# Second layer of an AdaLN and mixture-of-experts kernel: products of the dense expert cut in quarters, all gathers ahead of the scatters, two experts spread by matmuls

## What is computed

```python
def _L1_ffn_ref(x, Wg, W1, b1, W2, b2):        # x: 4 x 256 x 128, 8 experts, FF = 512
    n = b * l                                   # 1024 tokens
    k = min(max(int(n * C / e), 1), n)          # 256 tokens for each expert
    S = jax.nn.sigmoid(xt @ Wg).T
    G, I = jax.lax.top_k(S, k)                  # each expert takes its best 256 tokens
    ex = xt[I]
    hid = jax.nn.gelu(jnp.einsum('ekh,ehf->ekf', ex, W1) + b1[:, None, :], approximate=False)
    out = (jnp.einsum('ekf,efh->ekh', hid, W2) + b2[:, None, :]) * G[..., None]
    new_x = jnp.zeros_like(xt).at[I.reshape(-1)].add(out.reshape(-1, h))
    return new_x.reshape(b, l, h)
```

## Time and profile before

| what | value |
|---|---|
| median of 3 runs | 166.43 us (164.91 to 167.19) |
| the profiled execution | 165.73 us |
| its span, first to last instruction | 163.8 us |
| around the span | 1.93 us |
| PE busy in the span | 139.5 us (85%) |
| DVE, ACT, POOL busy | 90.4, 82.0, 61.8 us |
| mean granted clock of PE | 0.968 |

### The profile page before, as it was taken

The page is one execution under the profiler, slowest core; times in us unless marked ns, Lnnn a source line. Parts: engine busy times, 40 slices in busy tenths (PEclk is TensorE's granted clock), DMA queues, the critical chain, the costliest instruction groups (busy, mean ns, idle before and its releaser), DMA issues.

```text
span 163.8 us, 3459 instructions
## 1 busy us (share of the span) xinstructions
PE 139.5 (85%) x1050; PEld 120.0 (73%) x1050; DVE 90.4 (55%) x304; ACT 82.0 (50%) x246; POOL 61.8 (38%) x65
## 2 busy tenths in 40 slices
PE   7999839999998999997899787799889988699500
PEld 3848339999997999853889666689879868599500
DVE  0279564566543555333698877674414954357732
ACT  1677516667775666500586789631254553560000
POOL 0000376555375455444000000014775877764000
PEclk9999986999999999999999999999999999999965
DMA  5993315999997871117109904000212064366434
GB/s 163 375 401 116 81 50 164 411 388 386 392 384 222 245 281 33 36 48 216 42 0 363 397 14 136 0 6 17 51 51 55 32 180 109 117 179 171 130 117 128
DMA packets 20531, 27.38 MB, mean 167 GB/s; under 512 B 2050, under 2 KB 14722, under 8 KB 20130
## 3 DMA queue, kind: packets, MB, share of 16 engines
q1 hardware_dynamic: 17570, 22.78, 41.1%
q0 software_dynamic: 1856, 3.86, 7.6%
q10 hardware_dynamic: 1088, 0.52, 1.1%
HBM read 20.57 MB, written 6.59 MB: 166 GB/s over the span
## 4 chain that ended last, share of the span: by engine, by line
PE 50%; DMA 18%; DVE 10%; POOL 8%; issue 6%; ACT 5%; DVEq 1%; ACTq 0%; POOLq 0%
PE bank L561 12%; PE bank L571 10%; PE bank L723 6%; PE bank L705 5%; DMA xs<-rows,gidx 5%; POOL plane L450 4%; DMA plane<-x_sb,idx 3%; PE bank L473 3%; DMA w_sb<-plane 2%; DMA got<-picked 2%; DMA xg<-rows,idx 2%; PE bank L605 2%; POOL xg L443 2%; PE bank L681 2%; DMA rows<-c_tok 2%
## 5 line engine op out<-in xcount | busy, mean ns | idle before, releaser
L829 ACT ACTIVATE hT<-bank,w_now 128x128 f32<-128x128 f32 x92 | 26.2, 367 | 14.1 <-PE bank L561 14.1
L561 PE MATMUL bank<-xg,w_now 128*128 (+1 forms) x184 | 26.2, 289 | 0.0
L417 POOL DMA_INDIRECT xs<-rows,gidx x16 | 15.9, 991 | 27.3 <-DMA rows<-c_tok 18.3
L906 ACT ACTIVATE h1T<-bank,c_sb 128x256 f32<-128x256 f32 x44 | 18.3, 470 | 13.4 <-PE bank L705 13.4
L571 PE MATMUL bank<-w_sb,hT 128*128 (+1 forms) x184 | 24.5, 276 | 0.3 <-ACT hT L829 0.3
L561 PEld LDWEIGHTS bank<-xg,w_now 128*128 128x128 f32 x184 | 23.9, 203 | 0.4 <-issue 0.2
L723 PE MATMUL bank<-v_sb,h1T 128*128 128x128 f32 x176 | 22.7, 280 | 1.0 <-ACT h1T L906 1.0
L571 PEld LDWEIGHTS bank<-w_sb,hT 128*128 128x128 f32 x184 | 22.5, 192 | 0.5 <-ACT hT L829 0.5
L723 PEld LDWEIGHTS bank<-v_sb,h1T 128*128 128x128 f32 x176 | 21.2, 192 | 2.0 <-ACT h1T L906 1.7
L422 POOL DMA_INDIRECT picked<-y,sidx x16 | 15.3, 959 | 13.2 <-DVE y L1076 12.0
L450 POOL DMA_INDIRECT plane<-x_sb,idx x12 | 14.1, 1175 | 6.5 <-DVE x_sb L1235 4.1
(11 more groups left out here) (195 smaller groups left out, 216.1 us busy)
## 6 DMA issues: line engine op xcount, KB each, us to landing
v_sb<-in_v SPq DMA_DIRECT2D x16, 256.0 KB
cw_sb<-in_cond_w SPq DMA_DIRECT2D x8, 386.5 KB
plane<-y SPq DMA_DIRECT2D x6, 512.0 KB, 5.5
w_sb<-plane SPq DMA_DIRECT2D x6, 512.0 KB, 4.2
w_sb<-in_w SPq DMA_DIRECT2D x2, 1024.0 KB, 9.5
w_sb<-in_w SPq DMA_DIRECT2D x1, 1290.0 KB, 7.4
w_sb<-in_w SPq DMA_DIRECT2D x1, 774.0 KB, 4.3
rows<-row SPq DMA_DIRECT2D x1, 544.0 KB, 3.4
```

What stands on the lines that cost most here:

```text
L417: pool.indirect_dma_start(out=xs[:, b % RING], out_offset=None, in_=rows0, in_offset=rows_at(gidx, b)).then_inc(gathered[b % RING], 16)
L561: mm = pe.matmul(bank[2 + j % 2][:, P * f:P * f + P], w1_now[:, j % WB_RING, P * f:P * f + P], xsT[:, bass.ds((j - e) * P, P)], start=True ...
L829: ins = act.activation(hT[:, j % 2, P * f:P * f + P], bank[2 + j % 2][:, P * f:P * f + P], ACT.Relu, bias=w1_now[:, j % WB_RING, F + f:F + ...
L906: act.activation(h1T[:, n % 2, fc], bank[UP_BANKS[(2 * n + h) % 4]][:, CAP * f:CAP * f + CAP], ACT.Gelu, bias=c1_sb[:, e * NF + fc:e * NF ...
```

## The change

1. **Quarters.** `up1` can do one of its two matmuls alone. The two of `up1(0, 0)` go into the last two turns of the gated MLP's loop (b = 9 and 10). `up1(2, 0)`, `up1(2, 1)` and `up1(3, 0)` are halved, and the halves stand on the two sides of a `count_experts` or of `spread_tau`. The wait for the weights (`in_v`) moves ahead of the loop. The units' PSUM banks and those of `turn_scores` change with it.
2. **Order of the dense stage.** `up1(1, 1)`, `up1(2, 1)`, `down_e(0, 1)` stand earlier; `down_e(1, 0)` moves from ahead of `count_ahead` to behind it; `turn_xg(0)` moves ahead of `down_e(3, 1)` and `find_slots(4)`. On ACT `gelu(0, 0)` moves ahead of the 1024-wide pass (L921), `take_scores(1)` moves behind the fourth sign count, and ACT makes the first half of `hlfv`, which DVE made (L1203).
3. **Gathers.** All 14 gathers stand ahead of the first scatter.
4. **Experts 5 and 6 spread.** 5 planes in place of 6, 10 scatters in place of 12, 4 one-hot matrices and 4 x 8 matmuls of `spread_out` in place of 2 and 2 x 8. The planes are taken at `{4: 0, 5: 1, 6: 2}`.

The core of the diff:

```diff
-PLANES = 6
+SPREADS = 4
+PLANES = 5
@@
-        GATHERS_AHEAD = 5
+        GATHERS_AHEAD = SPARSE
+        SCATTERS = NH * SPARSE - SPREADS
+        SUM_BANKS = (5, 3)
@@
-        TAKEN_AT = {3: 0, 4: 1, 6: 2}
-        UP_BANKS = (4, 5, 2, 3)
+        TAKEN_AT = {4: 0, 5: 1, 6: 2}
+        UP_BANKS = (2, 4, 5, 3)
+        SCORE_BANKS = (0, 7)
@@ POOL, add(e)
-                for h in range(NH):
+                for h in range(min(NH, SCATTERS - NH * e)):
@@ PE
+            def up1(n, h, parts=(0, 1)):
...
+                for f in parts:
...
+            pe.wait_ge(in_v, 16 * 2 * E)
             for b in range(NC + 3):
...
+                if b > NC:
+                    up1(0, 0, (b - NC - 1,))
                 if 0 <= b - 3 < NC:
                     turn_d(b - 3)
@@ PE, spread_out
+                for n in range(SPREADS):
+                    e, h = (SCATTERS + n) // NH, (SCATTERS + n) % NH
+                    pe.wait_ge(spread_ready, n + 1)
                     pe.wait_ge(y1_kept, NH * e + h + 1)
@@ PE
-            up1(1, 0)
+            up1(1, 1)
+            up1(2, 0, (0,))
             count_experts(2)
+            up1(2, 0, (1,))
             down_e(0, 0)
             count_experts(3)
-            up1(1, 1)
+            down_e(0, 1)
+            up1(2, 1, (0,))
             count_experts(4)
-            down_e(0, 1)
+            up1(2, 1, (1,))
+            up1(3, 0, (0,))
             count_experts(5)
-            up1(2, 0)
             spread_tau()
+            up1(3, 0, (1,))
+            count_ahead()
             down_e(1, 0)
-            count_ahead()
...
@@ ACT
             take_scores(0)
+            gelu(0, 0)
             act.wait_ge(first_tau, 1)
             act.activation(rest, scT, ACT.Identity, bias=tau[:], scale=-1.0).then_inc(rest_ready, 1)
-            gelu(0, 0)
-            take_scores(1)
...
+            act.wait_ge(hlf1h_ready, 1)
+            act.activation(hlfv[:, :, :, 0].rearrange("p c e h -> p (c e) h"), hlf1h[:], ACT.Identity,
+                           scale=const("pcol")).then_inc(hlfv_ready[0], 1)
@@ DVE
-            v.wait_ge(hlf1h_ready, 1)
-            v.tensor_scalar(hlfv[:, :, :, 0].rearrange("p c e h -> p (c e) h"), hlf1h[:], const("pcol"), None,
-                            ALU.mult).then_inc(hlfv_ready[0], 1)
```

More of the change, by code:

```diff
@@ L394, in _ @@
             for e in range(PLANES):
-                sp.wait_ge(added[e], 16 * NH)
+                sp.wait_ge(added[e], 16 * min(NH, SCATTERS - NH * e))
                 load(part[e].rearrange("p (c d) -> p c d", d=C), plane[e].rearrange("(c p) d -> p c d", p=P), part_in[e])
@@ L626, in turn_d @@
                 pe.transpose(bank[6][:, 0:P], dT[:, P * b:P * b + P], ident).then_inc(d_turned, 1)
+            def up1(n, h, parts=(0, 1)):
+                dense, e, q = unit[n]
+                rows_in = dT[:, CAP * q:CAP * q + CAP] if dense else xgT[:, e % 2]
+                if not dense:
+                    pe.wait_ge(xgT_ready, e + 1)
+                u = 2 * n + h
+                if u >= 4:
+                    pe.wait_ge(h1T_ready, 2 * (u - 4) + 2)
+                for f in parts:
+                    fc = 2 * h + f
+                    mm = pe.matmul(bank[UP_BANKS[u % 4]][:, CAP * f:CAP * f + CAP], v1_sb[:, e, P * fc:P * fc + P],
+                                   rows_in, start=True, stop=True)
+                    if f == 1:
+                        mm.then_inc(h1_ready, 1)
             pe.wait_ge(in_gw, 32)
+            pe.wait_ge(in_v, 16 * 2 * E)
             for b in range(NC + 3):
@@ L644, in turn_scores @@
                     pe.wait_ge(scT_ready, c + 1)
-                    mm = pe.transpose(bank[2 + g][:, P * (c % 4):P * (c % 4) + P], scT[:, P * c:P * c + P], ident)
+                    mm = pe.transpose(bank[SCORE_BANKS[g]][:, P * (c % 4):P * (c % 4) + P], scT[:, P * c:P * c + P], ident)
                 mm.then_inc(s_turned, 1)
@@ L691, in turn_xg @@
                 mm.then_inc(xg_turned, 1)
[L693 to L707, removed]
             def down_e(n, h):
@@ L761, in _ @@
             find_slots(1)
-            up1(3, 1)
+            down_e(2, 1)
             find_slots(2)
-            down_e(2, 1)
+            down_e(3, 0)
             find_slots(3)
-            down_e(3, 0)
+            turn_xg(0)
+            down_e(3, 1)
             find_slots(4)
-            down_e(3, 1)
-            turn_xg(0)
             up1(HEAD, 0)
@@ L888, in take_scores @@
                 act.wait_ge(s_turned, g + 1)
[L889 removed]
+                first_of_each = bank[SCORE_BANKS[g]][:].rearrange("p (c e j) -> p c e j", c=4, j=NJ)[:, :, :, 0]
                 act.activation(sc[:, 4 * g:4 * g + 4], first_of_each, ACT.Copy)
@@ L929, in _ @@
             count_signs(4)
+            take_scores(1)
             count_signs(5)
@@ L1219, in spread_rows @@
                 v.wait_ge(iota_ready, 1)
-                link(v.tensor_copy(idx1f[:], idx1[:, PLANES * NH:SPARSE * NH]))
-                for h in range(NH):
-                    v.tensor_scalar(spread1h[h], iota_t, idx1f[:, h:h + 1], None, ALU.is_equal).then_inc(spread_ready, 1)
+                link(v.tensor_copy(idx1f[:], idx1[:, SCATTERS:NH * SPARSE]))
+                for n in range(SPREADS):
+                    v.tensor_scalar(spread1h[n], iota_t, idx1f[:, n:n + 1], None, ALU.is_equal).then_inc(spread_ready, 1)
             def with_bias(n, h):
@@ L1275, in _ @@
                 v.wait_ge(summed, g + 1)
-                v.tensor_tensor(acc[:, 512 * g:512 * g + 512], acc[:, 512 * g:512 * g + 512], bank[2 + g][:],
+                v.tensor_tensor(acc[:, 512 * g:512 * g + 512], acc[:, 512 * g:512 * g + 512], bank[SUM_BANKS[g]][:],
                                 ALU.add).then_inc(out_ready, 1)
```

32 lines of the change are left out of this document (15 added, 17 removed).

## The result

The changed kernel took 158.01 us in the median of 4 runs (157.73 to 158.72), the kernel before 165.94 us on the same chip (4 runs, 164.91 to 167.19). The ratio is 0.9526 with a 95% interval of 0.9446 to 0.9605. The profiled execution took 158.72 us with a span of 156.9. Forecast were 159.9 us for the median, with a range of 158.0 to 163.0, and 157.3 for the span.

The account below looks back on a forecast made before the run. PE's products and POOL's indirect DMAs bounded the kernel, POOL's last scatter setting the end. PE's end, 153.93 - 4.15 + 3.72 = 153.5, put the last addition 6.5 us earlier: span 157.3, execution 159.2, median 159.9 us, range 158.0 to 163.0.

Parts of the forecast that it names:

- signs that were named: Expected in the trace: no PE row waits from expert 3, first slots near 109.7, DVE's last addition released by PE.
- 157.9 us: Whole kernel: the low case, if the scatters are quick and the quarters give their full 0.95 us.
- Dense stage: After the last count: tau's turn, count_ahead and hlfv come earlier; first slots at 109.7, not 110.51, 0.8 us gained.
- rival C: Dense stage gives nothing, as a count or threshold is delayed; everything starts 0.8 us later, 160.7 us; chance 0.09.
- Gathers ahead: PE's expert turns: expert 2's 1.6 us earlier, expert 6's at 136.7 in place of 140.86, 4.15 us gained.
- More spreading: PE's tail: two more blocks of 16 records add 3.72 us, so PE ends at 153.5.
- Fewer scatters: POOL's tail: at 1.175 us each, the tenth scatter starts at 142.6 and its plane is added at 152.2.
- The rule weighed: GpSimd contends with DVE for SBUF, so two more wide one-hots beside scatters speak against the change; sum left unchanged.
- A: Tail: the scatters' route ends last, at 1.8 us from scatter to scatter; about 162.1 us as a median; chance 0.22.
- B: Gathers land after 4.0 us in place of 2.6, so all of PE comes 1.4 later; 161.3 us; chance 0.07.
- D: PE's clock falls at the wait ahead of expert 2's turn and stays down; at worst 192.7 us; chance 0.02.
- E: Tail: DVE's sum or the output's transfer doesn't move up although PE and POOL do; about 165 us; chance 0.05.

Follow-up runs that it names:

- e3: The kernel before with all gathers ahead and experts 5 and 6 spread, but the old dense stage: 159.64 us, ratio 0.9714.
- r0: The changed kernel run again, unedited, on a chip where the kernel before took 181.17 us: 170.46 us, ratio 0.95.
- e1: The changed kernel with the gathers of experts 5 and 6 behind scatters again and planes taken as before: 159.85 us, ratio 0.9707.
- e5: The kernel before with all gathers ahead of the scatters and planes taken as in the change, nothing else: 175.87 us, ratio 0.9752 (slower chip).
- e4: The kernel before with only the new dense stage; 5 gathers ahead, 6 planes, one expert spread: 164.27 us, ratio 0.9972.
- p1: The changed kernel with 5 unread matmuls, about 1.07 us, on PE ahead of the spreading: 171.16 us, ratio 0.9528 (slower chip).
- e2: The changed kernel with 6 planes, 12 scatters and only expert 6 spread: 162.64 us, ratio 0.987.
- e6: The kernel before with experts 5 and 6 spread and 5 planes, nothing else: 177.83 us, ratio 0.9867 (slower chip).

## Why the prediction was right

The order of events and the new bound came as forecast: the waits for the rows of experts 5 and 6 are gone, and PE's products bound the tail. One of the signs that were named didn't show in the first profile. DVE's last additions were to be released by PE and not by a plane's load; there the plane's load came last, by 0.05 us, while in e3 and r0 PE did. The median of 158.01 us lies 0.01 us inside the lower end of the range, which is luck. The 157.9 us that the working gives there for quick scatters and the full 0.95 us of the quarters doesn't follow from its own terms: with PE last, quick scatters give nothing, and 0.15 us more at the slots makes 159.8.

*Dense stage.* The order of the steps held, one size was off. The turn of `tau` was released at once, `count_ahead` came earlier, and ACT's `hlfv` was ready in time; the first slots came at 109.86 (forecast 109.7), counted from `thr` 0.9 us earlier than before (forecast 0.8). I then let the gather be the only thing that expert 2's turn waits for, which is true in the changed kernel (120.64, forecast 120.7). But the working priced rival C, "the dense stage gives nothing", at 0.8 us. e3 shows that undoing it costs 1.8: in the old order PE is late by its own work, and the gather's earlier landing wouldn't help. The gain of 1.6 us at that turn was in the sum; that both halves of it come from this part was not said.

*Gathers ahead.* The turn of expert 6 came at 136.71 against 136.7, with no wait of PE for the rows of experts 4 to 6: right. e1 loses 2.5 us without this part and e5 gains 2.5 us with it alone, near the 2.4 us of waits in the earlier trace rows.

*More spreading.* The 3.72 us added to PE's time were the right size or a little high: a block now takes 1.79 us from start to start (145.92 to 151.28 are three of them) and PE ends at 153.23 (forecast 153.5).

*Fewer scatters.* Here two errors cancel, and that is luck. The term "1.175 us on average" was too long: these ten have a median of 0.970 and a longest of 1.319 us. The three longest of before, 2.03, 1.71 and 1.25 us, stood beside wide additions of DVE, one of the dense expert's bias and two of planes. Beside the first of these stands a gather of 1.16 us now, and of the scatters only one is over 1.03. So the last scatter started at 141.29 and not at 142.6. The other way, landing and loading took longer than the 4.39 and 3.98 of the earlier trace rows: from the last scatter's issue to its plane's addition 10.03 us, forecast 8.37. The eighth scatter landed only after 6.68 us; SP, which takes the planes in order, then issued the loads of planes 3 and 4 together, and the second of them took 5.43. The plane was added at 152.55, forecast 152.2, and the 0.7 us of slack before PE became none in this profile; it was 0.95 in e3 and 1.48 in r0.

*The rule weighed.* Of the contention of GpSimd with DVE the traces say that a wide addition of two SBUF tensors can cost an issue up to 1.07 us (2.03 in place of 0.96), and that the one scatter of 1.32 us stands beside such an addition; the scatter ahead of it also does, over its last 0.4 us, and took 0.96. The four wide one-hots from 132.87 to 135.69 stand beside scatters of 0.96 to 1.03 us, so they cost POOL little here. But in the kernel before a scatter beside the two one-hots of the earlier trace rows took 1.24 us:

```profile
134.08 1.24 POOL L450 DMA_INDIRECT plane<-x_sb,idx  x1 [0.30 <-issue]
```

The same stands in e1 (131.65) and e4 (131.34). So the one-hots may cost POOL something too, and what sets the size isn't shown. The Trainium skill (GPSIMD Engine Reference, "Key points") names DVE instructions with two SBUF inputs or in a two-port mode; the traces agree on the first kind, and no run here shows in which mode the one-hots run.

*Rivals.* A drew level in one profile and was 0.95 and 1.48 us away in e3 and r0. B was right in its mechanism where gathers stand beside scatters (e1, 3.9 us). Its reason against, that only such gathers land late, did not hold in the changed kernel: with no scatter beside them the 8th, 9th and 12th gather landed after 4.4, 3.3 and 3.7 us. Only the 8th touched PE. The turn of expert 3 came 4.47 us behind that of expert 2 (4.28 in the kernel before), and at the turn of expert 4 that was made up. D didn't happen on the first chip (granted clock 1.00 from 92 to 150 us); on the second chip the clock did fall, as the last section shows, and what that cost isn't separated from the pause ahead of it. E is excluded: T fell with PE.

*The median.* 159.9 was 1.9 us too high. 0.4 us of it is the span (157.3 against 156.9), and 1.4 the distance between the profiled execution and the median: I had put it at +0.7 as before, and it was -0.7, since the profiled execution (158.72) was the highest of the four. That part was a guess about noise and not a term of the kernel, and so the 1.9 us aren't an error of the mechanism.

## What to carry to other kernels

When two queues share a tail, price both to the end and keep the margin between them: here one change moved the bound from POOL's scatters to PE's products and left 0.05 to 1.5 us between them. One profile with level routes doesn't say which of them is the bound; the same tail in another kernel (e3) and a known delay (p1) did. Move gathers ahead of scatters in an in-order queue when matmuls wait for the gathers. The first scatter came later by it, 129.68 us and not 126.48, but the last one came earlier: in e2 it is issued 16.8 us behind expert 4's turn, in e4, with gathers between the scatters, 19.3. Compare traces from a common event inside the stage, not from the start: with the same tail and PE as the bound stretch T repeated to 0.08 us where executions spread by 1 us and more. Look for pauses inside the stretch first (e6).

## What the runs showed beyond that

*Scatters that stand closer together landed later.* The scatters landed in 3.0 us in the median before and 3.5 after, at most 4.4 and 6.7; the plane loads' median went from 4.2 to 4.6. In the three profiles of the first chip with all gathers ahead (changed, e2, e3) the longest landing is 6.4 to 6.7 us, in the three others (before, e1, e4) 4.3 to 5.6. With the gathers ahead the scatters follow each other without other DMAs between them, and in the changed kernel landing and loading cost 1.7 us more than the latencies of the earlier trace rows. That scatters and plane loads delay each other is the likely reason; no run separates the two.

*The second chip.* In r0 DVE and ACT stand still with a releaser that the profile calls "remote", while POOL goes on issuing gathers (waits, 116 to 134 us: total, times, longest):

```profile
DVE idx L981 <- remote: 7.9, 2, 5.0
PEld bank L703 <- DVE slot1h L1218: 4.9, 2, 4.5
...
ACT xgT L907 <- remote: 3.9, 1, 3.9
```

PE then waits up to 4.1 us for DVE. The windows around it show PE's clock (columns as in the earlier trace rows):

```profile
124.00:128.00 4.00, 1.64 (x12) 1.18 (x12) 0.24 (x1) 0.38 (x1) 2.83 (x3) 0.88 0.22 52
128.00:132.00 4.00, 1.94 (x13) 1.77 (x14) 1.52 (x4) 1.22 (x3) 2.02 (x2) 0.50 0.14 35
132.00:136.00 4.00, 4.00 (x27) 3.50 (x26) 0.24 (x2) 1.95 (x5) 2.77 (x4) 0.77 0.25 56
```

PE is busy 1.64 and 1.94 of 4 us, the granted clock falls to 0.50, that is 1.2 GHz, and stays under 1.00 in the window behind it although PE works all of it. This is rival D's mechanism. The waits of 1.0 to 1.4 us for rows on the first chip didn't do it (granted clock 1.00 over them in the kernel before, e1 and e4). The Trainium skill, TensorE: Matmul & The Clock Gate, section "HAM oscillation — how this bites in real kernels", describes such a fall behind a long wait; the trace agrees for this pause. Against the first profile of the changed kernel `thr` comes 6.2 us later in r0 and S is 7.1 us longer, so this pause isn't all of the difference. What the engines waited for isn't shown, and no run here names the cause. The kernel before wasn't profiled on that chip; it took 180 us there, but that the same pauses stand in it is only likely.
